# Mamba scan on Trainium2: scan result kept in PSUM, six of sixteen products with C moved to GpSimd, softplus moved in VectorE's order

## The reference

```python
dt = jax.nn.softplus(jnp.einsum('blr,cr->blc', dt_in, dw) + db)
A = -jnp.exp(Alog)
def step(h, inp):
    dt_t, B_t, C_t, u_t = inp
    dA = jnp.exp(dt_t[..., None] * A)
    h = dA * h + (dt_t * u_t)[..., None] * B_t[:, None, :]
    y = jnp.einsum('bcn,bn->bc', h, C_t)
    return (h, y)
...
y = ys.transpose(1, 0, 2) + u * Dp
y = y * _silu(z)
```

## Time and profile before

| | |
|---|---|
| median of 3 runs | 2384.0 us (2383.7 to 2385.4) |
| profiled execution | 2378.9 us, its span 2376.9 us |
| loop of 240 rounds | from 92.7 to 876.2 us of the span |
| busy in the whole span | PE 77%, DVE 70%, ACT 56%, POOL 44% |
| granted TensorE clock over the span | 0.87 of full speed |

### The profile page before, as it was taken

How to read it: one execution, slowest core, us unless ns; L and a number is a source line. 1 busy time by engine, 2 the same in 40 slices (tenths; PEclk the granted TensorE clock), 3 DMA queues, 4 the chain that set the end, 5 groups by cost and what they waited for, 6 DMA issues and landing times. The chain is left out here.

```text
span 2376.9 us, 49583 instructions
## 1 busy us (share of the span) xinstructions
PE 1839.4 (77%) x19188; PEld 1360.2 (57%) x19188; DVE 1656.8 (70%) x2544; ACT 1326.2 (56%) x2658; POOL 1045.0 (44%) x811
## 2 busy tenths in 40 slices
PE   4788898888878765557647887777577599999997
PEld 3344444444433333335446777556566489999997
DVE  1599999999999983438295442326434478888886
ACT  2767777777767543013334444232355378888885
POOL 0377777777678750530005777200250023333332
PEclk8899999999999996558668999688687599999998
DMA  2344444444444421510025888300650231121000
GB/s 72 123 135 127 130 143 136 124 135 128 132 135 134 132 75 30 104 27 1 15 90 163 265 256 250 108 1 2 219 156 5 66 135 59 59 71 70 17 4 21
DMA packets 91293, 240.81 MB, mean 101 GB/s; under 512 B 16362, under 2 KB 39476, under 8 KB 88500
## 3 DMA queue, kind: packets, MB, share of 16 engines
q1 hardware_dynamic: 76612, 212.20, 28.7%
q0 software_dynamic: 9408, 18.93, 3.6%
q10 hardware_dynamic: 5040, 6.52, 0.8%
HBM read 222.30 MB, written 15.30 MB: 100 GB/s over the span
## 5 line engine op out<-in xcount | busy, mean ns | idle before, releaser
L874 POOL TENSOR_TENSOR dBu<-du,Bs 128x858 f32<-128x858 f32 (+1 forms) x240 | 588.2, 2453 | 228.5 <-DVE hst L798 101.5
L395 PE MATMUL py<-hst,ident 128*128 128x429 f32 (+1 forms) x960 | 415.6, 563 | 97.8 <-DVE hst L808 97.2
L798 DVE TENSOR_TENSOR_SCAN hst<-dA,dBu 128x858 f32<-128x858 f32 (+1 forms) x240 | 458.6, 1911 | 22.8 <-ACT dA L690 22.0
L1866 POOL DMA_INDIRECT xi<-token_rows,take x152 | 148.3, 976 | 542.5 <-POOLq L90 497.1
L690 ACT ACTIVATE dA<-dt,negA 128x416 f32<-128x416 f32 (+1 forms) x480 | 269.6, 596 | 185.5 <-DVE hst L798 184.1
L395 PEld LDWEIGHTS py<-hst,ident 128*128 128x128 f32 x960 | 183.6, 202 | 295.8 <-DVE hst L808 170.8
L2388 POOL TENSOR_TENSOR hm<-h,mw 128x264 f32<-128x264 f32 x128 | 90.4, 706 | 432.0 <-DVE h L2369 432.0
L808 DVE TENSOR_TENSOR hst<-hst,Cs 128x858 f32<-128x858 f32 (+1 forms) x240 | 247.5, 1031 | 0.0
L2284 PE MATMUL pg<-hs,wh 128*128 128x68 f16 x6144 | 215.2, 195 | 19.4 <-DVE hs L2372 16.3
L1961 ACT ACTIVATE eh<-ph,wb 128x128 f32<-128x128 f32 x480 | 136.8, 367 | 152.3 <-PE ph L1896 152.3
L2284 PE MATMUL pg<-xm,wi 128*128 128x68 f16 x6144 | 214.2, 195 | 4.5 <-issue 3.2
(11 more groups left out here) (395 smaller groups left out, 3364.8 us busy)
## 6 DMA issues: line engine op xcount, KB each, us to landing
wb<-sf_w SPq DMA_DIRECT2D x96, 514.0 KB, 4.8
Bs<-bc_rows SPq DMA_DIRECT2D x96, 429.0 KB, 4.7
Cs<-bc_rows SPq DMA_DIRECT2D x96, 429.0 KB, 3.5
mw<-route_weights SPq DMA_DIRECT2D x8, 2112.0 KB
wb<-gf_w SPq DMA_DIRECT2D x24, 514.0 KB, 5.0
Bs<-bc_rows SPq DMA_DIRECT2D x24, 396.0 KB, 5.0
Cs<-bc_rows SPq DMA_DIRECT2D x24, 396.0 KB, 4.3
mb<-route_masks SPq DMA_DIRECT2D x8, 1088.0 KB, 5.6
```

Source lines behind the costliest of these rows:

```text
L395: return nc.tensor.matmul(out, weight, moving, **kw)
L798: v.tensor_tensor_scan(hst[:, g % HR, 0:2 * n], dA[:, g % 2, 0:2 * n], dBu[:, g % 2, 0:2 * n], 0.0, ALU.mult, ALU.add).then_inc(h_ready, 1)
L874: g_.tensor_tensor(dBu[:, g % 2, 0:2 * n].rearrange("p (a n) -> p a n", a=2), du[:, j % 2, :, 0:n], Bs[:, q % NBS, k % BG, 0:n].unsqueeze( ...
L1866: pool.indirect_dma_start(xi[:, j % UN, :], None, xs, bass.IndirectOffsetOnAxis(ap=take[:, j:j + 1], axis=0)).then_inc(taken[j % UN][0], 16)
```

## The change

1. **Where the scan's result goes.** For k in `POOL_STATES` (0, 2, 5, 7, 10, 12) the scan still writes `hst`. For the ten other states it writes over dA, in PSUM, and VectorE multiplies from there into `hst`, now in the same round, right behind its own scan. ScalarE may overwrite a slot of dA only when that product is done (for the ten) or the scan (for the six).
2. **GpSimd takes six products.** `weigh(g-3)` of these states stands on GpSimd ahead of the product dBu of round g. dBu has three slots instead of two.
3. **The waits at k = 10 on GpSimd are gone.**
4. **VectorE's order.** The first instruction of the softplus (`series`) stands alone at k = 7, the other three at k = 10 behind `back`; `gate` goes from k = 1 to k = 2.
5. **The first token.** Instead of zeros kept in dA, dt is set to 1e28 at each sequence's first token (a memset of 26 or 24 elements a partition behind `du`), and the exponential of all 429 columns gives the zero.
6. **TensorE's additions** stand two rounds behind instead of one, and `hst` has 4 slots instead of 5.

```diff
-HR = 5
+HR = 4
+DB = 3
+POOL_STATES = (0, 2, 5, 7, 10, 12)
+def weighed_by(g):
+    p = sum(k in POOL_STATES for k in range(g % DST + 1)) + g // DST * len(POOL_STATES)
+    return g + 1 - p, p
...
# TensorE
-                pe.wait_ge(weighed, g + 1)
+                if k in POOL_STATES:
+                    pe.wait_ge(weighed_pool, weighed_by(g)[1])
+                else:
+                    pe.wait_ge(weighed, weighed_by(g)[0])
...
-                if g >= 1:
-                    add(g - 1)
+                if g >= 2:
+                    add(g - 2)
...
# ScalarE
                 if g >= 2:
-                    act.wait_ge(h_ready, g - 1)
+                    if (g - 2) % DST in POOL_STATES:
+                        act.wait_ge(h_ready, g - 1)
+                    else:
+                        act.wait_ge(weighed, weighed_by(g - 2)[0])
                 for h in range(2):
-                    o = by_seq(dA[:, g % 2, h * n:h * n + n])[:, :, 1:S]
-                    last = a(o, by_seq(dt[:, j % 2, h, 0:n])[:, :, 1:S], ACT.Exp,
+                    last = a(dA[:, g % 2, h * n:h * n + n], dt[:, j % 2, h, 0:n], ACT.Exp,
...
# VectorE
+                dve.wait_ge(du_done, j + 1)
+                starts = dt[:, j % 2, :, 0:n].rearrange("p a (b s) -> p a b s", s=S)[:, :, :, 0]
+                v.memset(starts, CUT).then_inc(dt_cut, 1)
...
-                if g >= HR:
-                    dve.wait_ge(y_added, g - HR + 1)
                 dve.wait_ge(dBu_ready, g + 1)
                 dve.wait_ge(dA_ready, g + 1)
-                v.tensor_tensor_scan(hst[:, g % HR, 0:2 * n], dA[:, g % 2, 0:2 * n], dBu[:, g % 2, 0:2 * n], 0.0, ALU.mult,
-                                     ALU.add).then_inc(h_ready, 1)
+                d = dA[:, g % 2, 0:2 * n]
+                o = d
+                if g % DST in POOL_STATES:
+                    o = hst[:, g % HR, 0:2 * n]
+                    if g >= HR:
+                        dve.wait_ge(y_added, g - HR + 1)
+                v.tensor_tensor_scan(o, d, dBu[:, g % DB, 0:2 * n], 0.0, ALU.mult, ALU.add).then_inc(h_ready, 1)
...
-                if g >= 1:
-                    weigh(g - 1)
...
+                if k not in POOL_STATES:
+                    weigh(g)
-                if j >= 1 and k == 1:
+                if j >= 1 and k == 2:
                     gate(j - 1)
-                if k == 8:
+                if k == 7 and j + 1 < NI:
+                    series(j + 1)
+                if k == 10:
+                    if j >= 2:
+                        back(j - 2)
                     if j + 1 < NI:
                         soften(j + 1)
-                    if j >= 2:
-                        back(j - 2)
...
# GpSimd
-                if k == 10:
-                    if j + 1 < NI:
-                        pool.wait_ge(du_done, j + 2)
-                    if j >= 2:
-                        pool.wait_ge(m_scaled, j - 1)
+                if (k - 3) % DST in POOL_STATES and g >= 3:
+                    weigh(g - 3)
...
-                if g >= 2:
-                    pool.wait_ge(h_ready, g - 1)
+                if g >= DB:
+                    pool.wait_ge(h_ready, g - DB + 1)
```

More of the change, by code:

```diff
@@ L253 @@
 NGR = DST // BG
-HR = 5
+HR = 4
[4 more added lines that the diff above has]
+    return g + 1 - p, p
 SER_A, SER_B, SER_C = 0.5673937377696069, -0.44049436669574327, 0.8059644831764592
 PER_ITEM = 3
+CUT = 1e28
 LSTM_ITEMS = S // PER_ITEM
@@ L301, in mamba_lstm @@
         Cs = sb("Cs", [128, NBS, BG, SCW])
-        dBu = sb("dBu", [128, 2, 2 * SCW])
+        dBu = sb("dBu", [128, DB, 2 * SCW])
         hst = sb("hst", [128, HR, 2 * SCW])
@@ L327, in mamba_lstm @@
             stage(nc, "d_ready e_abs d_read e_ready ser_ready ln_ready marked ser_done patched dt_done du_done"))
-        (dA_zeroed, dBu_ready, dA_ready, h_ready, weighed, y_added, y_gated) = ctx.enter_context(
-            stage(nc, "dA_zeroed dBu_ready dA_ready h_ready weighed y_added y_gated"))
+        (dt_cut, dBu_ready, dA_ready, h_ready, weighed, weighed_pool, y_added, y_gated) = ctx.enter_context(
+            stage(nc, "dt_cut dBu_ready dA_ready h_ready weighed weighed_pool y_added y_gated"))
         (wop_ready, wop_kept, cent_ready, cent_kept, sq_ready, var_ready, var_kept, var_logged, rstd_ready, m_scaled, m_done) = ctx.enter_context(
@@ L384, in _ @@
                     if q >= NBS:
-                        sp.wait_ge(weighed, BG * (q - NBS + 1))
+                        sp.wait_ge(weighed, weighed_by(BG * (q - NBS + 1) - 1)[0])
+                        if weighed_by(BG * (q - NBS + 1) - 1)[1] > 0:
+                            sp.wait_ge(weighed_pool, weighed_by(BG * (q - NBS + 1) - 1)[1])
                     sp.dma_start(Cs[:, q % NBS, :, 0:n], rows(j, DST, k)).then_inc(c_loaded[q % NBS], 16)
@@ L540, in _ @@
                     lstm(PER_ITEM * (j + 1))
+            add(NI * DST - 2)
             add(NI * DST - 1)
@@ L728, in _, with series @@
             v.memset(xd[DTR + 2 * DST:DTR + 2 * DST + 1, :, :], 1.0).then_inc(ones_set, 1)
-            v.memset(dA[:, :, :], 0.0).then_inc(dA_zeroed, 1)
             v.memset(cz[:, 1, :], 0.0)
-            def soften(j):
+            def series(j):
                 l, at, n = item(j)
@@ L736, in soften @@
                 v.scalar_tensor_tensor(out=t, in0=t, scalar=SER_C, in1=e[:, :, 0:n], op0=ALU.add, op1=ALU.mult).then_inc(ser_done, 1)
+            def soften(j):
+                l, at, n = item(j)
+                t = ser[:, :, 0:n]
                 dve.wait_ge(ln_ready, j + 1)
@@ L804, in weigh @@
                 q = g // BG
+                dve.wait_ge(c_loaded[q % NBS], 16 * (q // NBS + 1))
+                if g >= HR:
+                    dve.wait_ge(y_added, g - HR + 1)
                 dve.wait_ge(h_ready, g + 1)
-                dve.wait_ge(c_loaded[q % NBS], 16 * (q // NBS + 1))
-                h = hst[:, g % HR, 0:2 * n].rearrange("p (a n) -> p a n", a=2)
-                v.tensor_tensor(h, h, Cs[:, q % NBS, k % BG, 0:n].unsqueeze(1).broadcast_to([128, 2, n]),
+                h = dA[:, g % 2, 0:2 * n].rearrange("p (a n) -> p a n", a=2)
+                v.tensor_tensor(hst[:, g % HR, 0:2 * n].rearrange("p (a n) -> p a n", a=2), h, Cs[:, q % NBS, k % BG, 0:n].unsqueeze(1).broadcast_to([128, 2, n]),
                                 ALU.mult).then_inc(weighed, 1)
+            series(0)
             soften(0)
@@ L858, in _, with weigh @@
             g_.tensor_tensor(lb[:, 0, :], lb[:, 0, :], lb[:, 1, :], ALU.add).then_inc(bias_set, 1)
+            def weigh(g):
+                j, k = g // DST, g % DST
+                l, at, n = item(j)
+                q = g // BG
+                pool.wait_ge(c_loaded[q % NBS], 16 * (q // NBS + 1))
+                pool.wait_ge(h_ready, g + 1)
+                h = hst[:, g % HR, 0:2 * n].rearrange("p (a n) -> p a n", a=2)
+                g_.tensor_tensor(h, h, Cs[:, q % NBS, k % BG, 0:n].unsqueeze(1).broadcast_to([128, 2, n]),
+                                 ALU.mult).then_inc(weighed_pool, 1)
             for g in range(NI * DST):
@@ L864, in _ @@
                     pool.wait_ge(du_done, j + 1)
-                if k == 10:
-                    if j + 1 < NI:
-                        pool.wait_ge(du_done, j + 2)
-                    if j >= 2:
-                        pool.wait_ge(m_scaled, j - 1)
+                if (k - 3) % DST in POOL_STATES and g >= 3:
+                    weigh(g - 3)
                 if g % BG == 0:
                     pool.wait_ge(b_loaded[q % NBS], 16 * (q // NBS + 1))
-                if g >= 2:
-                    pool.wait_ge(h_ready, g - 1)
-                g_.tensor_tensor(dBu[:, g % 2, 0:2 * n].rearrange("p (a n) -> p a n", a=2), du[:, j % 2, :, 0:n],
+                if g >= DB:
+                    pool.wait_ge(h_ready, g - DB + 1)
+                g_.tensor_tensor(dBu[:, g % DB, 0:2 * n].rearrange("p (a n) -> p a n", a=2), du[:, j % 2, :, 0:n],
                                  Bs[:, q % NBS, k % BG, 0:n].unsqueeze(1).broadcast_to([128, 2, n]), ALU.mult).then_inc(dBu_ready, 1)
```

4 lines of the change are left out of this document (1 added, 3 removed).

## The result

The changed kernel takes 2423.3 us in the median of 4 runs (2418.2 to 2426.4), the kernel before 2383.9 in 4 runs beside it. The ratio is 1.0165 with a 95% interval of 1.0145 to 1.0186, so the change costs 39 us. The forecast was 2394 with a range to 2414: the direction was right, the size too small by 29 us.

What follows compares the result with a forecast made beforehand. VectorE was taken to set the loop's time, with TensorE next. The terms, -83 + 4 + 15 + 9 + 4 + 5 + 43 + 13 = +10 us, gave 2394 us on the runs' scale, range 2356 to 2414.

Steps and rivals of the forecast that it cites:

- Products taken off VectorE: Loop: six products in each of 15 items leave VectorE, -83 us together.
- Memsets: VectorE in the loop: 14 memsets of 26 elements with a wait before each, 0.3 us each, +4 us.
- Product behind its own scan: VectorE's rounds: a product dependent on the scan just before costs 0.13 us more, 117 times, +15 us.
- PSUM as source and as target: VectorE: products reading PSUM 1.5 us, left out; scans writing PSUM taken as nothing, range -7 to +15 us.
- Rival C: VectorE's scans: writing into PSUM is dearer by 0.1 us each, 2409 us; chance 0.10.
- GpSimd in the softplus: Softplus chain: two GpSimd products come in between VectorE's dependent instructions, 3.1 us in each of 14 items, +43 us.
- Rival A: Softplus: GpSimd doesn't get in between VectorE's chained instructions, or comes late; 43 us go, 2351 us; chance 0.15.
- D: Loop: rival in which GpSimd becomes the bound, 54 us an item against 52, some 2410 us; chance 0.03.
- Gates at k = 1 and 9: `lstm_c` on VectorE waits for ScalarE's gates: 9 us at k = 1, 4 us at k = 9.
- scan 5: Scan 5 waits for TensorE's addition of state 1, about 0.5 us in 11 items with LSTM, +5 us.
- TensorE's clock: Behind the softplus: half clock on rounds 11 to 14 costs 0.9 us in 14 items, +13 us, ends 0 and 17.
- Rival B: TensorE makes up its clock loss before anyone waits for it, 2381 us; chance 0.20.

Runs made afterwards that it cites:

- e6: e1 with POOL_STATES empty, so all 240 products are on VectorE behind their own scans: 2446.8 us, ratio 1.0271.
- held kernel: The changed kernel with GpSimd made to wait before its product 10 until the next item's dt*u is done (e1): 2375.3 us.
- e2: The kernel before, with VectorE's product of each state directly behind that state's own scan, all in SBUF: ratio 1.0137, loop 819.6 us.
- e9: The changed kernel with the wait for the scan written first, so that VectorE's product itself holds it: ratio 1.0161, loop 823.4 us.
- e13: The changed kernel with the edits of both e3 and e9: ratio 1.0043, loop 794.1 us.
- e1: The changed kernel with GpSimd made to wait before its product 10 until the next item's dt*u is done: 2375.3 us, ratio 0.9965.
- e3: The changed kernel with twelve more matmuls of zeros an item on TensorE, ahead of the addition of state 10: 2398.7 us, ratio 1.0065.
- e5: The kernel before with the product behind its own scan, in SBUF, and the changed kernel's three waits in their order: 2595.5 us, ratio 1.0898.
- e11: The changed kernel with all scan results in SBUF and the wait for the scan in the product itself: ratio 1.0445, loop 899.8 us.

## Why the prediction was right in kind and wrong in size

- **Products taken off VectorE, -83.** Not measurable alone. e6 gives 80.4 us for the share in the held kernel, where each product also has its link and hides part of other waits. The size is right, in part by luck.
- **Memsets, +4.** L772 takes 0.08 us, and from the start of du to the scan it is 1.17 us, where du's successor came after 0.97 before: 3 us.
- **Product behind its own scan, +15.** The 0.13 us hold with the wait in the product (e2). In the changed kernel the wait sits in an instruction of its own, which the forecast had not looked for: 0.24 x 117 = 28 us of rounds. Taking these 13 us away gave nothing in e9 and 6 us in e13.
- **PSUM as source and as target, 0.** L837 1.04, L826 1.91 for both targets. Right, and with it the choice of the gate's row over the 62 cycles that the prediction had from the Trainium skill, "VectorE: DVE Perf Modes", section on the TRN2 errata. Rival C falls.
- **GpSimd in the softplus, +43.** Two blocks, on patch and dt in most items, 41.3 us by e1. Right. One small block was missed: L753, the series at k = 7, which the prediction held to be out of GpSimd's reach, takes 1346 ns instead of 1046, some 4 us, in e1 too. Rival A falls with e1; D falls with it too, since GpSimd could be held for 5.78 us an item and the kernel was faster.
- **Gates at k = 1 and 9, +13; scan 5, +5; TensorE's clock, +13.** These 31 us are the step that failed. The list of waits has 21.2 us for the gates and 33.4 us for additions, 52 us more than before. e3, where the clock stays up, takes them apart:
  - The gates cost 11.1 us there, so the +13 were right.
  - Scan 5 was mis-sized. The prediction had VectorE 0.5 us early; with the full clock round k = 4 still takes 0.93 us more than without LSTM work, 10 us in 11 items. Item 0 has another 3.2 us, in e3 as in the changed kernel, whose cause no run isolates.
  - The clock gives back 24.2 us, where the forecast had 13 with 17 as its end. The prediction let TensorE make up 2.5 of 3.4 us before the next item and the rest come out at scan 0 or at the gates; round k = 1 gives back 10.1 us, near that. What it left out is a second low stretch, at k = 3, exactly ahead of the addition that scan 5 needs: 1.7 us in each of nine items, 15 us in the changed kernel. e3 wins 10.0 at k = 4, since two of its items still have a low stretch there. The remaining 4.2 us are at k = 15, where the product of state 15 waits for the addition of state 11. The prediction knew the low stretch behind the softplus only.
  - The stall there lasts 8.0 us in item 7. That it grew by the softplus's 3 us was in the prediction; that TensorE waits in it for ScalarE's copy `xd` at k = 14 was not.

Rival B, that nobody waits, falls.

The terms as measured, with the -83 left as forecast and the small block at k = 7 added, give -83 + 3 + 28 + 41 + 4 + 52 = +45 us, and stand against a loop that is 40.4 us longer. The parts overlap, as e9 shows, and I can't assign the 5 us between the two. That the forecast had the direction right rests on the main term, which was right; that it missed the size rests on the waits.

## What to carry to other kernels

When an engine's stall is made longer, follow the engine that waits behind it to each place where someone waits for it, and read its clock there too: here half a clock was paid at k = 1, at k = 4 and at k = 15, and the forecast had the first alone. Hold GpSimd wherever VectorE runs a chain of instructions with both inputs in SBUF; one wait was worth 46 us here. And an edit that shortens rounds is worth nothing while another engine is late, as e9 was; it has to be tried together with the cure for that.

## What the hardware showed that I had not expected

- The wait for an instruction's predecessor costs 0.034 us behind the scan if the waiting instruction holds it, and 0.133 us if a semaphore instruction ahead of it does (e2 against e5, e9 against the changed kernel), in SBUF and PSUM alike.
- Where the scan's end releases GpSimd too, this 0.1 us often decided who came first: e5, which differs from e2 in the waits ahead of the product alone, takes 178 us more. In e11 the short gap brought only 7 us of the loop.
- Work without effect made the kernel faster: 12 matmuls, 8.9 us in each item's stall, brought 24 us, while the low clock fell from 153.6 to 17.1 us.
